# Row fills of the pair tiles: from four whole transfers in the setup to eight halves beside the subtractions of sets two to five

## What is computed

```
L0: x = x + softmax(q k^T / sqrt(16)) v       q from layernorm(x), k and v from layernorm(ctx); 8 heads
L1: x = x + masked softmax(q k^T / sqrt(8)) v  k and v from ctx; 16 heads, causal and padding masks
L2: x = x + attention(x, ctx) @ Wo + bo;  x = x + gelu(x @ W1 + b1) @ W2 + b2          16 heads
L3: x = layernorm(x + masked self-attention @ Wo1);  x = layernorm(x + cross-attention @ Wo2)
    x = layernorm(x + gelu(x @ W1) @ W2)                                               16 heads
```

## Time and profile before

| | |
|---|---|
| median of 3 runs | 497.14 us (496.58, 497.14, 505.9) |
| the profiled execution | 495.54 us, its span 493.8 us, 1.74 us around it |
| busy: PE, DVE, ACT, POOL | 91%, 78%, 65%, 47% of the span |
| chain that ended last | PE 76%, DVE 10%, DMA 4%, issue 3%, ACT 2%, POOL 2% |
| granted TensorE clock | 0.96 in the mean; in the first four slices of 12.3 us 0.9, 0.6, 0.5, 0.7 |
| PE busy in the same slices | 0.3, 0.4, 0.7, 0.8 |
| DMA | 40.48 MB, mean 82 GB/s; first slices 125 and 167 GB/s |

### The profile page before, as it was taken

How to read it: one execution, slowest core, us unless ns; L and a number is a source line. 1 busy time by engine, 2 the same in 40 slices (tenths; PEclk the granted TensorE clock), 3 DMA queues, 4 the chain that set the end, 5 groups by cost and what they waited for, 6 DMA issues and landing times.

```text
span 493.8 us, 17187 instructions
## 1 busy us (share of the span) xinstructions
PE 447.9 (91%) x6720; PEld 302.8 (61%) x6720; DVE 386.2 (78%) x1099; ACT 321.9 (65%) x660; POOL 234.2 (47%) x290
## 2 busy tenths in 40 slices
PE   3478989899999998899999999999999999999981
PEld 2365656556666665577767666666666666666761
DVE  6587897778878878889988877888889987877552
ACT  2345765457676667678777676667677787777841
POOL 6246576856734534454554444334444543222345
PEclk9657998899999999999999999999999999999997
DMA  7644343643433444433433322222244341220001
GB/s 125 167 101 104 91 102 82 142 115 87 106 84 93 111 110 98 101 93 94 91 77 62 68 51 68 68 69 69 53 86 94 76 93 47 63 56 14 14 23 32
DMA packets 71579, 40.48 MB, mean 82 GB/s; under 512 B 7896, under 2 KB 70584, under 8 KB 71500
## 3 DMA queue, kind: packets, MB, share of 16 engines
q1 hardware_dynamic: 69280, 36.04, 30.2%
q0 software_dynamic: 2112, 3.24, 4.7%
q10 hardware_dynamic: 108, 0.10, 0.1%
HBM read 4.74 MB, written 1.05 MB: 12 GB/s over the span
## 4 chain that ended last, share of the span: by engine, by line
PE 76%; DVE 10%; DMA 4%; issue 3%; ACT 2%; POOL 2%; SPq 1%; POOLq 0%; DVEq 0%; ACTq 0%
PE attn_ps L1016 17%; PE o_ps L1043 15%; PE misc_ps L1073 6%; PE misc_ps L1064 5%; PE misc_ps L978 5%; PE misc_ps L1050 4%; PE score_ps L897 4%; PE misc_ps L984 3%; PE misc_ps L979 3%; DVE max_words L823 3%; PE misc_ps L1056 2%; DVE normed_in L759 2%; PE misc_ps L995 2%; DMA c_tok<-in_ctx_dram 2%; PE score_ps L930 2%
## 5 line engine op out<-in xcount | busy, mean ns | idle before, releaser
L823 DVE TENSOR_REDUCE max_words<-score_ps 128x4 f32<-128x512 f32 x288 | 193.7, 683 | 50.5 <-PE score_ps L930 47.6
L703 ACT ACTIVATE probs<-attn_ps 128x512 f32<-128x512 f32 x288 | 169.7, 601 | 74.4 <-PE attn_ps L1016 68.5
L1016 PE MATMUL attn_ps<-pairs 55*128 55x128 bf16 (+1 forms) x1152 | 113.7, 220 | 9.0 <-DMA pairs<-max_rows 3.4
L930 PE MATMUL score_ps<-pairs 52*128 52x128 bf16 (+1 forms) x1152 | 115.4, 222 | 2.3 <-DMA pairs<-terms 2.0
L560 POOL TENSOR_TENSOR rest<-qk_f,terms 128x512 f32<-128x512 f32 x38 | 44.2, 1162 | 114.2 <-ACT terms L654 114.2
L1016 PEld LDWEIGHTS attn_ps<-pairs 55*128 55x128 bf16 (+1 forms) x1152 | 64.9, 95 | 53.3 <-issue 26.8
L1043 PE MATMUL o_ps<-probs,v 128*32 128x128 f32 x2304 | 96.8, 281 | 0.1
L930 PEld LDWEIGHTS score_ps<-pairs 52*128 52x128 bf16 (+1 forms) x1152 | 67.3, 96 | 6.5 <-DMA pairs<-terms 2.8
L1043 PEld LDWEIGHTS o_ps<-probs,v 128*32 128x32 f32 x2304 | 53.5, 109 | 23.4 <-issue 9.5
L568 POOL TENSOR_TENSOR terms<-rest,terms 128x512 bf16<-128x512 f32 x38 | 44.0, 1158 | 9.7 <-DVE max_words L836 7.2
L712 ACT ACTIVATE o_sb<-o_ps 128x256 f32<-128x256 f32 x80 | 30.9, 386 | 23.7 <-PE o_ps L1043 22.7
(11 more groups left out here) (121 smaller groups left out, 751.0 us busy)
## 6 DMA issues: line engine op xcount, KB each, us to landing
pairs<-terms SPq DMA_DIRECT2D x240, 128.0 KB
x_tok<-in_x_dram SPq DMA_DIRECT2D x8, 128.0 KB, 2.6
c_tok<-in_ctx_dram SPq DMA_DIRECT2D x8, 128.0 KB, 3.0
pairs<-max_rows SPq DMA_DIRECT2D x64, 12.0 KB
w<-in_weights_dram POOLq DMA_DIRECT2D x8, 128.0 KB, 3.2
out_dram<-x_tok SPq DMA_DIRECT2D x8, 128.0 KB, 1.8
w<-in_weights_dram POOLq DMA_DIRECT2D x5, 192.0 KB, 3.3
pairs<-template POOLq DMA_DIRECT2D x4, 112.0 KB, 7.9
```

The costliest lines, as they stand in the source:

```text
L703: act.activation(probs[n % PROBS_RING][:, :, :].rearrange("p h q -> p (h q)"), attn_ps[n % 2][:, :], ACT.Exp, scale=float(D // HEADS[part] ...
L823: dve.tensor_reduce(max_words[ub(step) % 2][:, QUAD * g:QUAD * (g + 1)], score_ps[n % 2][:, :].rearrange("p (h k) -> p h k", h=QUAD), AX_X ...
L930: return pe.matmul(score_ps[NUM[step] % 2][:, j * S:(j + 1) * S], tile[score_rows(u), QUAD * g + j, 0, b * S:(b + 1) * S], tile[score_rows ...
L1016: last = pe.matmul(attn_ps[n % 2][:, j * S:(j + 1) * S], pairs[attn_rows(u), h, 1, b * S:(b + 1) * S], pairs[attn_rows(u), h, 0, b * S:(b ...
```

## The change

fill_rows takes a range of heads now and copies eight of the sixteen (56 KB). It is called eight times: behind GpSimd's instruction of step rest (heads 0 to 7) and behind that of step term2 (heads 8 to 15) of units 2 to 5, for places 0 to 3. The four calls in the setup and in step ln_in of unit 0 are gone. Each place has a semaphore of its own, and GpSimd waits for that of the set ahead of its mask rows. SP's wait ahead of unit 8 is gone.

```
-            fill_rows(pool, 0)
-            fill_rows(pool, 1)                                # end of the setup
...
-                    pool.wait_ge(fill16_landed, 16 * RING)
+                    pool.wait_ge(fill16_landed[u], 32)        # step mask, u < 4
...
                 if step.kind == "ln_in" and u == 0:
-                    fill_rows(pool, 2)
-                    fill_rows(pool, 3)
...
+                if step.kind in ("rest", "term2") and SPLIT_BY_DVE <= u < SPLIT_BY_DVE + RING:
+                    if u == SPLIT_BY_DVE:
+                        pool.wait_ge(rows_ready, 3)
+                    fill_rows(pool, u - SPLIT_BY_DVE, slice(0, 8) if step.kind == "rest" else slice(8, 16))
...
-                        if u == SETS:                         # SP, step stack, c == 0
-                            sp.wait_ge(fill16_landed, 16 * RING)
```

More of the change, by code:

```diff
@@ L304, in build @@
         mask_landed = [sem(f"mask_landed{r}") for r in range(RING)]
-        fill16_landed = sem("fill16_landed")
+        fill16_landed = [sem(f"fill16_landed{r}") for r in range(RING)]
         misc_ready = sem("misc_ready")
@@ L379, in the, with fill_rows @@
             return Step(kind, u, b, g)
-        def fill_rows(pool, r):
+        def fill_rows(pool, r, heads):
             first = product_rows(SETS)
             rows_ = slice(HALF * (r % 2) + first, HALF * (r % 2) + first + MASK_ROWS + TERMS)
-            pool.dma_start(pairs16[r // 2][rows_, :, :, :].rearrange("p h a n -> p h (a n)"),
+            pool.dma_start(pairs16[r // 2][rows_, heads, :, :].rearrange("p h a n -> p h (a n)"),
                            template[first:first + MASK_ROWS + TERMS, :, :, :].rearrange("p a b n -> p (a b n)")
-                           .unsqueeze(1).to_broadcast([MASK_ROWS + TERMS, 16, 2 * TOK])).then_inc(fill16_landed, 16)
+                           .unsqueeze(1).to_broadcast([MASK_ROWS + TERMS, 8, 2 * TOK])).then_inc(fill16_landed[r], 16)
         def mask_rows(pool, u):
```

## The result

The changed kernel takes 505.6 us in the median of 4 runs (500.58, 505.08, 506.12, 506.44). The kernel before, run beside it, takes 501.52 us (496.58, 497.14, 505.9, 506.92). The ratio is 1.0163, 95% interval [1.0115, 1.0211]. I forecast 492 and a gain of 4.7 us; by this ratio the change loses 8 us.

What follows compares the result with a forecast made beforehand. The first 70 us were taken to be bound by set 1's c_tok load (11.50 us), slowed by the four fills. Terms -4.5 - 0.8 + 0.6 + 0 = -4.7 us gave 492 us, range 487.5 to 497.

Steps and rivals of the forecast that it cites:

- Fills leave the start: At the start: c_tok of set 1 lands earlier, so DVE begins ln_in 1 at 10.76 instead of 15.26, 4.5 us gained.
- Eight issues on GpSimd: Units 2 to 5: issues of 0.66 us each hide in GpSimd's waits; taken as 0, bound 0.3 us lost.
- A gap between rest and term1: Units 3 and 4: DVE's normalising runs free during the issue, 0.4 us gained each, 0.8 in all; bounds 0 and 1.7.
- The halves' own transfers: Units 2 and 3: halves delay the two exposed max_rows, 0.3 us each, 0.6 lost in all; range 0 to 2.7.
- Does the shift last?: After the start: semaphores release everything, nothing goes by time of day, so the 4.5 us carry to the end.
- Clock: TensorE's granted clock, sets 0 to 3: taken as 0; up to 3 us gained, or 1 lost by a relapse elsewhere.
- fills in front of max_rows: Rival: halves landing after 7.9 us hold both exposed max_rows, 7.5 us lost, 500 us in all; chance 0.07.

Runs made afterwards that it cites:

- d1: The changed kernel with 64 more waits on an already raised semaphore at the start of TensorE's program; ratio 1.0142, 0 of 6 under 499.5 us.
- d2: The changed kernel with 96 more waits on an already raised semaphore at the start of TensorE's program; ratio 1.0191, 0 of 6 under 499.5 us.
- a3: The kernel before with each fill cut in two halves at its old place in the setup; ratio 1.0015, 2 of 12 under 499.5 us.
- a1: The changed kernel itself, timed again against the kernel before; median 507.57 us, ratio 1.0218.
- c2: The changed kernel once more, for more times against the kernel before; ratio 1.0188, 0 of 6 under 499.5 us.
- b1: The changed kernel with both halves of a place behind term2 and none behind rest; ratio 0.9978, 6 of 10 under 499.5 us.
- c1: The changed kernel with both halves behind term2 and a DVE memset of 512 columns inside normalising of units 3 and 4; ratio 0.9954.
- e2: The changed kernel with the heads cut 15 to 1 instead of 8 to 8; ratio 0.9972, 8 of 12 under 499.5 us.
- e1: The changed kernel with fifteen heads behind rest and one head of each place in the setup; ratio 0.999, 6 of 13 under 499.5 us.
- b2: The changed kernel with four whole fills behind rest and none behind term2; ratio 0.9947, 7 of 9 under 499.5 us.
- c3: The changed kernel with four whole fills behind rest, timed again; ratio 0.9959, 10 of 12 under 499.5 us.
- a2: The changed kernel with four whole fills behind term2 and none behind rest; ratio 0.9933, 3 of 6 under 499.5 us.
- c4: The changed kernel with four whole fills behind term2, timed again; ratio 0.9914, 6 of 8 under 499.5 us, lowest 490.54 us.
- d4: Four whole fills behind term2, with 64 more waits at the start of TensorE's program; ratio 0.9916, 2 of 6 under 499.5 us.
- d3: The kernel before with 64 more waits at the start of TensorE's program, as a control; ratio 1.0015, 4 of 6 under 499.5 us.
- a4: The changed kernel with DVE held 4.3 us by memsets ahead of ln_in 1; median 500.18 us, ratio 1.0085.
- b3: The kernel before with added matrix products in units 6 to 9 where TensorE waits; median 503.8 us, ratio 1.0151.
- b4: The changed kernel with added matrix products in units 6 to 9 where TensorE waits; median 501.52 us, ratio 1.0079.

## Why the prediction was wrong

*Fills leave the start*: right. 4.5 us were forecast, DVE begins 4.63 us earlier (10.63 against 15.26) and the first exponential comes 4.17 us earlier. c_tok, which took 11.50 us, is off the chain, and no issue of SP stalls.

*Eight issues on GpSimd*: right. They take 0.62 us each, and up to 74 us nothing is late behind them but what the next point names.

*A gap between rest and term1*: wrong in sign. I took -0.8; it is +0.72 in unit 3 and +0.67 in unit 4, 1.4 us. I had bounded it by 0 on the side of loss, as if an issue that holds DVE just as arithmetic does could cost nothing. But the trace of before already has the two slow instructions end less than 0.1 us behind rest and term1 (33.47 and 34.59 against 33.39 and 34.50): DVE stands there until GpSimd's operation is over. In order of time, before, the first pair (its second instruction is the slow one):

```profile
32.03 1.44 DVE L759 TENSOR_SCALAR normed_in<-x_tok,mean_var,rstd 128x128 f32<-128x128 f32 x2
32.17 1.21 POOL L560 TENSOR_TENSOR rest<-qk_f,terms 128x512 f32<-128x512 f32 x1 [0.19 <-ACT terms L654]
```

With an issue in between, the one that started as rest ended stands for that too, while GpSimd's issue keeps its usual length. The prediction drew on the Trainium skill (SBUF — State Buffer, "Who interferes with whom") for GpSimd's descriptor writing being starved, and by that the sum was -5.6 us. The same section also says that whoever issues first holds the shared pair and the other blocks. So it leaves room for DVE as the one that waits, which is what these traces show (1.91 us instead of 1.19); my reading took one half of it.

*The halves' own transfers*: mis-sized. I took +0.6 with up to 2.7; both exposed max_rows are unchanged, since the halves land in 2.9 to 3.9 us. What I had not thought of comes at 74 us, when they are long done: the mask transfer of that time lands 0.4 us or more later. What that alone costs isn't shown.

*Does the shift last?* This is the step that failed: carrying the 4.5 us to the end, with the clock at 0. The lead was there until 74 us, and the passage from L0 to L1 then took 14.7 us more, some 13.7 of them by the clock. "Nothing by the time of day" is true of semaphores, but not of two things that the traces show: the granted clock, and which transfers of three queues meet. *Clock* was sized 0, and a relapse 1, because I looked at sets 0 to 3 alone, where the chain was. The clock rows of before already held 6.8 us of half clock at 75 to 96 us, and two groups of times, 497 and 505.9, stood in the three runs shown: I read the third as scatter. The rival that ends slower (fills in front of max_rows, 500 us) had an event that does occur in d1, d2 and a3, a small transfer behind GpSimd's, but at another time and with the mask rows in front. That after came out slower by another way gives this rival no support.

**What is shown and what is open.** Under 499.5 us lay, with all times of a program taken together, those beside the result too:

```
cut and place                                          under 499.5
8 to 8, rest and term2 (after, a1, c2, d1, d2)            0 of 28
8 to 8, both behind term2 (b1, c1)                       14 of 24
8 to 8, in the setup (a3)                                 2 of 12
15 to 1, rest and term2 (e2)                              8 of 12
15 behind rest, 1 in the setup (e1)                       6 of 13
whole, behind rest (b2, c3)                              17 of 21
whole, behind term2 (a2, c4, d4)                         11 of 20
whole, in the setup (before, d3)                         50 of 118
```

(a4, b3, b4, which hold an engine up or busy, are left out.) Shown is that the loss lies at half clock between L0 and L1, that halves of eight heads together with the issue behind rest and the early start brought times over 500 us in all 28 runs (a4, which gives up the early start, escapes most of it), and that with the other cut, or with both halves behind term2, the same early start keeps the lower group. Whether halves alone make it rarer (a3, 2 of 12) is not settled by so few times. Shown is also that the late stack of unit 6 isn't the cause by itself (d1, d2, and b1, where TensorE waits 2.52 us for it and the clock stays full until 91 us). Not shown is why the even cut makes a mask transfer later, and why the combination tips the clock every time. a2's profiled run has the short waits of c3 and still lies in the upper group (its clock falls at 82.2 us), so the idle times at units 5 and 6 don't decide it; whether they make the fall likelier is open. A test that sets those waits one by one wasn't tried.

## What to carry to other kernels

Before carrying a gain at the start to the end, look along the whole trace for stretches at the lower granted clock and ask whether the shift, or any transfer that moves, adds idle time to the bound engine there. If the times of a kernel fall in groups, count the groups before and after an edit: a3's median was 507.76 us at a ratio of 1.0015. A DMA issue put between two GpSimd operations isn't free for DVE; put it where DVE isn't normalising, as behind term2 here, and try it in one piece first. (Whole fills behind term2 had the lowest times, 490.5 us; that they also had fewer slow passages than before, 11 of 20 times under 499.5 against 50 of 118, is within chance.)

## What the runs showed of the hardware

- A normalising instruction of VectorE's that starts just as GpSimd's subtraction ends, with a DMA issue of GpSimd's next, stood through the issue and the subtraction behind it, and ended 0.09 us after that: 1.91 and 1.86 us instead of 1.19, with the issue at 0.68 and 0.63.
- With the cut of four fills of 112 KB goes the time in which a mask transfer issued 10 us and more later lands: 4.6 to 6.5 us where they are cut 8 to 8 heads (ten kernels), 4.0 to 4.2 where they are whole or cut 15 to 1 or 1 to 15 (ten kernels), whatever their place and number. Why is open.
- A 16 KB fetch of TensorE's code can hold back the last completions of a 128 KB transfer: 5.66 to 6.08 us instead of 3.95 to 4.56. It went away with 64 or 96 waits ahead of the code (4.32 and 4.45), with the fetch now 2 us and more ahead of the transfer's issue.
- The same passage took 14.7 us more when 34.1 us of it ran at 1.2 GHz instead of 6.8, and a kernel whose source is unchanged falls on either side of it (44 of 108 times on the better one).
